# Norms, the recurrence and the routing laid between the units of two mixtures of experts, in a four-block Trainium2 kernel

## What is computed

```python
x = x + 0.5 * moe(layernorm(x));  x = x + rwkv(layernorm(x));  x = x + 0.5 * moe(layernorm(x))
x = x + 0.5 * ffn(layernorm(x));  x = x + attention(layernorm(x));  x = x + 0.5 * ffn(layernorm(x))

def moe(x):                                   # 8 experts, hidden size 512, the two best of a token
    logits = x @ router_w + router_b
    gates = softmax(logits where among the top 2, else -1e30)
    h = relu(x @ w1[e] + b1[e]);  y = h @ w2[e] + b2[e]
    return sum over e of gates[:, e] * y      # every expert is computed for every token

def rwkv(x):                                  # along the 2048 tokens, for each of 128 channels
    k, v, r = mixes of x[t] and x[t-1], times Wk, Wv, Wr
    q = max(p, u + k); e1 = exp(p - q); e2 = exp(u + k - q); y = (e1*a + e2*v) / (e1*b + e2)
    q2 = max(p + w, k); f1 = exp(p + w - q2); f2 = exp(k - q2); a, b, p = f1*a + f2*v, f1*b + f2, q2
    return (sigmoid(r) * y) @ Wo
```

## Time and profile before

| | us |
|---|---|
| median of 3 runs (2172.72 to 2175.76) | 2174.58 |
| the profiled execution | 2179.51 |
| its span, first to last instruction | 2177.7 |
| PE busy in it | 2010.9 |
| DVE busy | 1852.0 |
| ACT busy | 1521.1 |
| POOL busy | 1414.8 |

### The profile page before, as it was taken

One profiled execution on the slowest core, in us unless ns is written; L12 is line 12 of the kernel. 1 busy time (PEld: TensorE's weight loads), 2 busy tenths in 40 slices (PEclk: granted clock), 3 DMA queues, 4 the chain that ended last, 5 costly groups with the idle time before them and its releaser, 6 DMA issues. The chain is left out here.

```text
span 2177.7 us, 25650 instructions
## 1 busy us (share of the span) xinstructions
PE 2010.9 (92%) x8288; PEld 1438.4 (66%) x8288; DVE 1852.0 (85%) x2001; ACT 1521.1 (70%) x1873; POOL 1414.8 (65%) x660
## 2 busy tenths in 40 slices
PE   5999638999869999999999999999999999999877
PEld 4888427887546766766766676676766667666545
DVE  5888886887677999899899899989989989999885
ACT  4666435665417878788788787877878888788753
POOL 1000010000308999899989989989998998999872
PEclk6999758998779999999999999999999999999987
DMA  2210002110050303123031231312313122130000
GB/s 105 76 49 30 0 0 60 49 49 15 4 116 6 71 15 74 28 55 76 13 74 31 52 67 23 73 20 62 69 21 68 30 58 57 31 69 17 5 1 20
DMA packets 77272, 94.68 MB, mean 43 GB/s; under 512 B 31755, under 2 KB 35211, under 8 KB 76870
## 3 DMA queue, kind: packets, MB, share of 16 engines
q1 hardware_dynamic: 77142, 93.04, 18.8%
HBM read 41.11 MB, written 1.42 MB: 20 GB/s over the span
## 5 line engine op out<-in xcount | busy, mean ns | idle before, releaser
L490 POOL TENSOR_TENSOR p_l<-p_raw,p_h 128x1024 fp32r<-128x1024 f32 x512 | 1241.8, 2457 | 148.1 <-ACT p_h L1068 133.2
L1065 ACT ACTIVATE p_raw<-ps 128x1024 f32<-128x1024 f32 x512 | 567.2, 1108 | 241.7 <-PE ps L711 240.9
L1387 DVE TENSOR_REDUCE m_part<-ps 128x1 f32<-128x1024 f32 x480 | 584.9, 1218 | 125.7 <-PE ps L688 124.7
L1068 ACT ACTIVATE p_h<-ps 128x1024 fp32r<-128x1024 f32 x512 | 523.4, 1022 | 0.0
L710 PE MATMUL ps<-qa,ka 128*128 128x512 f32 x1024 | 445.8, 435 | 2.0 <-ACT m_t L1036 2.0
L711 PE MATMUL ps<-qb,kb 65*128 65x512 f32 x1024 | 409.2, 400 | 0.0
L725 PE MATMUL ps<-p_h,v_hl 128*128 128x512 f32 x1024 | 402.6, 393 | 1.1 <-POOL p_l L490 0.9
L1381 DVE TENSOR_REDUCE l_sum<-p_raw 128x128 f32<-128x1280 f32 x256 | 377.2, 1477 | 0.4
L688 PE MATMUL ps<-ka,qa 128*128 128x512 f32 x960 | 314.9, 409 | 12.6 <-DVE m_part L1387 12.4
L728 PE MATMUL ps<-p_l,v_hl 128*64 128x512 f32 x1024 | 321.3, 395 | 0.0
L1367 DVE TENSOR_REDUCE p_raw<-p_raw 128x128 f32<-128x1024 f32 x256 | 309.2, 1209 | 12.2 <-ACT p_raw L1065 12.2
(11 more groups left out here) (187 smaller groups left out, 2653.4 us busy)
## 6 DMA issues: line engine op xcount, KB each, us to landing
big<-g_scratch SPq DMA_DIRECT2D x64, 256.0 KB, 3.2
xnp<-r_scratch SPq DMA_DIRECT2D x59, 256.0 KB, 3.9
qa<-qk_hi SPq DMA_DIRECT2D x112, 128.0 KB, 2.3
ka<-qk_hi SPq DMA_DIRECT2D x56, 128.0 KB, 2.4
kb<-qk_hi SPq DMA_DIRECT2D x56, 128.0 KB, 2.4
ka<-xnp SPq DMA_DIRECT2D x28, 128.0 KB, 2.4
...
```

The lines of the kernel that those rows point to most:

```text
L490: nc.gpsimd.tensor_tensor(p_l[:, g % 4, :, :], slots(g), p_h[:, g % 4, :, :].bitcast(fp32), ALU.subtract).then_inc(pl_done, 1)
L1065: af(slots(g), s_t, ACT.Exp).then_inc(raw_done, 1)
L1068: af(p_h[:, g % 4, :, :], s_t, ACT.Exp).then_inc(ph_done, 1)
L1387: nc.vector.tensor_reduce(m_part[:, it, half:half + 1], ps[:, 4:6, :].rearrange("p b n -> p (b n)"), AX.X, ALU.max).then_inc(s_max, 1)
```

## The change

`layer_norm(0)` to `moe(1)` become one function on each engine, `mixtures()`. It counts ticks t from -16 to 265. At tick t of 0 to 255 stand the first product of unit t (256 units, both mixtures in one row) and the second product of unit t - 4. All other work is cut into pieces for one chunk and tied to ticks by tables: `ROUTE_AT` gives for each of the 8 chunks of routing (with its norm) the tick at which it begins, `RWKV_AT` the same for the 4 chunks of recurrence (with theirs), `WEIGHTS_AT` for the split of each expert's weights, and `N_...`, `R_...`, `K_...`, `W_...` say how many ticks later each piece stands. The scans run over 512 tokens and hand their last column to the next chunk.

- b1 goes into the first product: the last channel of the normed x, which is minus the sum of the others, is replaced by a row of ones, w1 by its difference to its last row (`w1_base`, one more load, and one DVE instruction per expert), and the last row of w1 by b1 (`b1_row`, moved by a DMA behind the weight loads).
- `h_raw` is gone: ACT writes relu(ps) as the high part itself, for every unit (`high_hidden`), and DVE takes max(ps, 0) minus that (`low_hidden`), so both read the PSUM bank.
- DVE gates and adds each expert's output (`gate_expert`, `add_expert`); the half is in the gates.
- The low parts of the weights, of x, and five products of the recurrence per chunk are POOL's.
- Weights are loaded in four parts and split expert by expert; x's first chunk is loaded ahead of them.

```diff
+TICKS = 2 * NC * UNITS
+TAIL = LAG + 6
+HEAD_START = 16
+NORMS = ((0, 0), (0, 1), (0, 2), (1, 0), (0, 3), (1, 1), (2, 0), (1, 2), (2, 1), (1, 3), (2, 2), (2, 3))
+ROUTE_AT = (-16, 0, 20, 59, 95, 131, 167, 187)
+RWKV_AT = (40, 76, 112, 148)
+WEIGHTS_AT = (-8, -5, 2, 6, 10, 14, 18, 22)
+WEIGHT_PARTS = ((0, 1), (1, 2), (2, 4), (4, 8))
+N_MEAN, N_CEN, N_SQR, N_VAR, N_STD, N_REC, N_SPREAD, N_OUT = 0, 1, 1, 4, 5, 6, 8, 9
+R_HIGH, R_LOGITS, R_LOW, R_TOP, R_SECOND, R_EXP, R_GATES, R_TURN, R_ROWS = 10, 11, 11, 12, 13, 14, 15, 18, 19
+K_DIFF, K_MIX, K_PROJECT, K_EVICT = 10, (11, 12, 13), (13, 14, 16), (14, 15, 17)
+K_MAX, K_F1, K_F2, K_Q, K_E1, K_E2 = 15, 16, 17, 18, 19, 20
+K_EXP = (18, 19, 20, 21)
+K_FV, K_EV, K_SCAN_B, K_SCAN_A, K_DEN, K_DEN2 = 20, 22, 21, 22, 23, 24
+K_LN, K_INV, K_EA, K_NUM, K_GATE, K_NR, K_NR2, K_OUT, K_PROJECT_OUT, K_ADD = 25, 26, 24, 25, 26, 27, 28, 29, 32, 33
+W_BASE, W_HI, W_LO, W2_HI, W2_LO = 0, 1, 1, 2, 3
 
 
 def macaron_kernel(nc, a, out, g_scratch, l_scratch, r_scratch):
@@ -76,9 +93,7 @@
...
+            def load_weights(i):
+
+                lo, hi = WEIGHT_PARTS[i]
+                sp.dma_start(w1_raw[0:C - 1, lo:hi, :], a["w1T"][0:C - 1, lo:hi, :]).then_inc(w1_loaded[i], 16)
+                sp.dma_start(w1_base[0:C - 1, lo:hi, :],
+                             a["w1T"][C - 1:C, lo:hi, :].to_broadcast([C - 1, hi - lo, H0])).then_inc(w1_loaded[i], 16)
+                sp.dma_start(w2_raw[:, lo:hi, :, :], a["w2T"][:, lo:hi, :, :]).then_inc(w2_loaded[i], 16)
...
+            load_weights(3)
+            sp.wait_ge(b1_done, 1)
+            sp.dma_start(w1_raw[C - 1:C, :, :].rearrange("p e n -> p (e n)"), b1_row[:, :]).then_inc(b1_moved, 16)
...
+                    if at == R_LOGITS:
+                        pe.wait_ge(small_loaded, 16 * 3)
+                        pe.wait_ge(ln_out, norm_index(k, c) + 1)
...
+            def first_product(t):
+                j, u = t // UNITS, t % UNITS
+                e, ht = u // HT0, u % HT0
+                if t == 0:
+                    pe.wait_ge(row_loaded, 16)
+                if u == 0:
+                    pe.wait_ge(xl_done, j + 1)
+                if j == 0 and ht == 0:
+                    pe.wait_ge(w_lo, e + 1)
+                if t >= 4:
+                    pe.wait_ge(h_done, t - 3)
+                cols = slice(ht * 128, ht * 128 + 128)
+                split_product(ps[:, t % 4, :], w1_h[:, e, cols], w1_l[:, e, cols], x_h[:, chunk(j % NC)], x_l[:, chunk(j % NC)],
+                              True, True).then_inc(h_ps, 1)
+
+            def second_product(t):
+                n, ht = t // HT0, t % HT0
+                e = n % E
+                if ht == 0 and n < E:
+                    pe.wait_ge(w2_lo, e + 1)
+                if ht == 0 and n >= 2:
+                    pe.wait_ge(y_gate, n - 1)
+                pe.wait_ge(h_done, t + 1)
+                split_product(ps[:, 4 + n % 2, :], w2_h[:, e, ht, :], w2_l[:, e, ht, :], h_h[:, t % 4, :], h_l[:, t % 4, :],
+                              ht == 0, ht == HT0 - 1).then_inc(w2_done, 1)
...
-                    for u in range(UNITS):
-                        e, ht = u // HT0, u % HT0
-                        act.wait_ge(h_ps, at * UNITS + u + 1)
-                        act.wait_ge(h_done, PRIME + at * UNITS + max(u - 3, 0))
-                        af(h_raw[:, u % 4, :], ps[:, u % 4, :], ACT.Relu, bias=b1[:, e, ht:ht + 1]).then_inc(h_relu, 1)
-                        if u % 2 == 1:
-                            act.wait_ge(h_relu, PRIME + at * UNITS + u)
-                            act.wait_ge(w2_done, PRIME + at * UNITS + max(u - 4, 0))
-                            af(h_h[:, (u - 1) % 4, :], h_raw[:, (u - 1) % 4, :], ACT.Copy).then_inc(h_hi, 1)
...
+            def high_hidden(t):
+                act.wait_ge(h_ps, t + 1)
+                if t >= 4:
+                    act.wait_ge(w2_done, t - 3)
+                af(h_h[:, t % 4, :], ps[:, t % 4, :], ACT.Relu).then_inc(h_hi, 1)
...
-                    for u in range(0, UNITS, 2):
-                        v = u + 1
-                        dve.wait_ge(h_relu, PRIME + at * UNITS + v + 1)
-                        dve.wait_ge(w2_done, PRIME + at * UNITS + max(v - 3, 0))
-                        nc.vector.tensor_copy(h_h[:, v % 4, :], h_raw[:, v % 4, :]).then_inc(h_hi2, 1)
-                        dve.wait_ge(h_hi, at * (UNITS // 2) + u // 2 + 1)
-                        low(u)
-                        dve.wait_ge(h_hi2, at * (UNITS // 2) + u // 2 + 1)
-                        low(v)
...
+            def low_hidden(t):
+
+                dve.wait_ge(h_hi, t + 1)
+                stt(h_l[:, t % 4, :], ps[:, t % 4, :], 0.0, h_h[:, t % 4, :].bitcast(fp32), ALU.max, ALU.subtract).then_inc(h_done, 1)
+
+            def gate_expert(n):
+
+                j, e = n // E, n % E
+                dve.wait_ge(w2_done, HT0 * (n + 1))
+                dve.wait_ge(g_loaded[e], 16 * (j + 1))
+                stt(y_gated[:, n % 2, :], ps[:, 4 + n % 2, :], b2[:, e:e + 1], g_bc[:, e, :], ALU.add, ALU.mult).then_inc(y_gate, 1)
+
+            def add_expert(n):
+
+                cols = chunk(n // E % NC)
+                dve.wait_ge(y_gate, n + 1)
+                if n % E > 0:
+                    dve.wait_ge(y_add, n)
+                tt(x[:, cols], x[:, cols], y_gated[:, n % 2, :], ALU.add).then_inc(y_add, 1)
...
+                    elif at == K_EA:
+                        pool.wait_ge(wkv_a, c + 1)
+                        nc.gpsimd.tensor_tensor(w_num, w_e1, a_sum[:, 0:CH], ALU.mult).then_inc(pool_step, 1)
+                    elif at == K_NUM:
+                        pool.wait_ge(pool_step, 2 * c + 1)
+                        pool.wait_ge(wkv_prod, 2 * c + 2)
+                        nc.gpsimd.tensor_tensor(w_num, w_num, w_ev, ALU.add).then_inc(pool_step, 1)
+                    elif at == K_GATE:
+                        pool.wait_ge(pool_step, 2 * c + 2)
...
+                    elif at == K_SCAN_A:
+                        step(nc.vector.tensor_copy(a_sum[:, 0:1], a_sum[:, CH:CH + 1]) if c > 0 else nc.vector.memset(a_sum[:, 0:1], 0.0))
+                        dve.wait_ge(wkv_prod, 2 * c + 1)
+                        nc.vector.tensor_tensor_scan(a_sum[:, 1:CH + 1], w_f1, w_fv, a_sum[:, 0:1] if c > 0 else 0.0, ALU.mult, ALU.add).then_inc(wkv_a, 1)
+                    elif at == K_DEN:
+                        dve.wait_ge(wkv_exp, 4 * c + 3)
+                        step(tt(w_den, w_e1, b_sum[:, 0:CH], ALU.mult))
...
+            def mixtures():
+                dve.wait_ge(const_ready, CONST)
+                for t in range(-HEAD_START, TICKS + TAIL):
+                    if 0 <= t < TICKS:
+                        low_hidden(t)
+                    n = (t - LAG - HT0) // HT0
+                    if t % HT0 == 0 and 0 <= n < 2 * E * NC:
+                        gate_expert(n)
+                    if t % HT0 == 1 and 0 <= n < 2 * E * NC:
+                        add_expert(n)
+                    base_weights(t)
+                    route(t)
+                    rwkv(t)
```

More of the change, by code:

```diff
@@ new lines, in route @@
+            def route(t):
+                for j, base in enumerate(ROUTE_AT):
+                    at, k, c = t - base, 2 * (j // NC), j % NC
+                    norm(k, c, at)
+                    if at == R_LOGITS:
+                        pe.wait_ge(small_loaded, 16 * 3)
+                        pe.wait_ge(ln_out, norm_index(k, c) + 1)
+                        for i in range(TPC):
+                            tile = slice(c * CH + i * 128, c * CH + i * 128 + 128)
+                            last = mm(ps[:, 7, E * (i + 1):E * (i + 2)], xn[:, tile], rw[:, :], start=True, stop=True)
+                        last.then_inc(rt_logits, 1)
+                    elif at == R_TURN:
+                        pe.wait_ge(rt_gates, j + 1)
+                        outs = sum(b + K_PROJECT_OUT < t for b in RWKV_AT)
+                        if outs > 0:
+                            pe.wait_ge(rwkv_added, outs)
+                        for i in range(TPC):
+                            last = mm(ps[0:E, 7, i * 128:i * 128 + 128], gates[:, i, :], ident[:, :], start=True, stop=True)
+                        last.then_inc(gt_ps, 1)
@@ new lines, in mixtures @@
+            def mixtures():
+                pe.wait_ge(const_ready, CONST)
+                pe.wait_ge(b1_loaded, 16)
+                mm(ps[0:UNITS, 5, 0:128], b1[:, :], ident[:, :], start=True, stop=True).then_inc(b1_ps, 1)
+                for t in range(-HEAD_START, TICKS + TAIL):
+                    if 0 <= t < TICKS:
+                        first_product(t)
+                    if 0 <= t - LAG < TICKS:
+                        second_product(t - LAG)
+                    route(t)
+                    rwkv(t)
@@ L895, in attention @@
                 end_out(NC, 5)
[L897 to L902 removed]
+            mixtures()
             layer_norm(3)
@@ new lines, in high_hidden, with mixtures @@
+            def high_hidden(t):
```

(11 more changed lines are left out.)

576 lines of the change are left out of this document (305 added, 271 removed).

## The result

The changed kernel takes 2300.48 us (median of 4 runs, 2297.61 to 2304.51); the kernel before took 2175.17 us beside it (4 runs, 2172.72 to 2181.26). The ratio is 1.057, 95% interval 1.055 to 1.060: 125 us slower. The forecast was 2125 us, range 2098 to 2158, with 0.93 for faster. It was wrong in its sign.

What follows compares the result with a forecast made beforehand. PE bounds the mixtures, a chain across engines, mostly DVE, the stretch between them. Start 31 + clock 3 + PE 407 + waits 31 = 472 instead of 523.5; 50 us net gain gives 2125 us, own range 2108 to 2144, eight in ten 2098 to 2158.

Steps and rivals of the forecast that it cites:

- The start: Head before the mixtures: weights at 335 GB/s, b1 lands near 26.5, first unit at 31 us (28 to 35), before 50.4.
- The rival on the same spot: Head: b1's DMA of 32 short rows late, first unit near 45, 14 us more, 2139; included in the forecast's 0.56.
- PE's own sum: Mixtures from tick 0: 256 units of six matmuls 349 us, pieces laid in 58, together 407 us with nothing waiting.
- The slower rival: Mixtures: DVE's `low_hidden` costs more than 0.60, slower than before from 1.1 us each, 2190 at 1.15; slower 0.05.
- The locks: Recurrence: POOL and DVE exclude each other, DVE held 4.5 us per chunk, bounds 0 and 6.3.
- The waits: PE inside the mixtures: logits 10 us plus 5.1 per recurrence chunk, 31 us in all, bounds 8 and 75.
- The logits' wait: Mixtures: PE's logits stand one tick behind DVE's `N_OUT`; wait 1.5 us, seven times, 10 us.
- The low clock: Head: PE, idle some ten us, comes back at 1.2 GHz; 3 us added (0 to 6).
- The end: Behind the mixtures: fourth norm's variances 5.1 us after the last product, 1.3 given back; attention and both ffn same instructions.
- The signs: Would show it wrong: mixtures' clock below 0.95, idle PE in plain ticks (205 to 255), `low_hidden` over 0.8.

Runs made afterwards that it cites:

- with 128 rows: Changed kernel with both first-layer weight loads over 128 partitions instead of 127, b1's row waiting for them: 2153.64 us, ratio 0.992 to the kernel before.
- with the products on DVE: Kernel with 128-row loads, POOL's five recurrence products per chunk given to DVE in the same ticks, nothing left out: 2139.78 us in one run.
- with short ones: Kernel with 128-row loads, POOL's five recurrence products cut to 8 columns, the recurrence's output left out: 2132.06 us in one run.

## Why the prediction was wrong

**The start** is the step that failed: "7.1 MB at 335 GB/s is 21 us, so b1 lands near 26.5". The rate was taken from loads with 128 partitions and used for loads with 127. Measured, they go at 25 to 28 GB/s; the term of 31 us came out as 179.5. This error of 148.5 and the 26 by which the stretch behind it runs over (467 for 441) make 174.5, the miss of 175. The mechanism, one DMA engine of sixteen for 127 rows, is shown by four runs with other row counts and by the share of busy engines in them. Its bounds of 28 and 35 rested on the same unspoken step, that the row count doesn't matter, for which no row of before spoke; it should have widened the range. Everything else in that step held: with 128 rows the first unit starts at 33.05, 2 us behind the forecast.

**The rival on the same spot** ("the first unit starts near 45, since b1's DMA is late") named the wrong transfer. b1's row is late because of the loads ahead of it, and 14 us was a tenth of the lateness. With 128 rows ahead of it, the same 32 short rows landed 2.5 us behind their issue.

**PE's own sum** held: 1.36 for a unit where nothing is laid in, forecast 1.364.

**The slower rival** (`low_hidden` "costs more than 0.60") was wrong in its mechanism. DVE's low part takes 0.69 alone and 0.60 behind another, and DVE has 96.8 us idle before it (with 128 rows). That the kernel did get slower (0.05 in the chances) had another cause.

**The locks** came out at 3.9 us of DVE per chunk, forecast 4.5: three products at 1.04, 1.04 and 0.73 too much, and the additions at 64 x 0.067 = 4.3 over all chunks. The Trainium skill's rule ("SBUF — State Buffer", section "SBUF: two separate sides") of a lock held for one whole instruction fits these rows: every held DVE product ends 0.55 us behind the one POOL instruction that it met, and none is held for a second; by it three waits of 1.27 were 3.8. The run of three in the earlier trace rows, which was weighed against it, doesn't recur where POOL waits for a semaphore between its instructions.

**The waits** were named in the wrong places. The logits' wait, forecast at 10 us, is 0 in the changed kernel. The norm's spread, not forecast, waits 15.9 us in four chunks, for a reciprocal on DVE; the locks make 5 to 7 us of that (11.2 with the products on DVE, 8.8 with short ones), and what makes the rest is not taken apart. PE's waits sum to 33 us with 128 rows (15.9 spread, 5.3 variances, 4.8 low parts, 3.3 turns, 2.1 projection, 1.7 at the first variances), forecast 31: the total was right by two errors that cancel.

**The low clock** was counted once, 3 us at the start, and there it held (matmuls 0.43 apart from 33.05 to 37.45, some 2 us lost). The term had nothing for the mixtures, where the clock falls too (with 128 rows eight times, each in a wait of PE's or within 2 us behind one): 15.5 us are lost in the stretch with 128 rows, 11.0 in the changed kernel. With 128 rows it is 469.5 us from the first unit to the end of the last product, forecast 472 less 31 = 441. Of the 28.5 over, some 15 are clock and 2 waits; the rest, 11 or 12, is not taken apart by any run here (the logits' piece costs 1.1 where 0.87 was taken, the turn 1.2 for 1.0, some 3 us in all).

**The end** held: the fourth norm's variances were forecast 5.1 us behind the last product; it is 5.1 (646.47 to 651.58), and all behind is unchanged but for 3 us (1647.1 for 1650.5).

**The signs** that were to show the forecast wrong, a clock below 0.95 in the mixtures (it was 0.97), idle PE in plain ticks (60.00 of 60 us busy) and a low part over 0.8 (0.69), all stayed away, though it was wrong in its sign. All three look at the mixtures; of the loads nothing but the first unit's start would have told.
